# Cross-attention block on one core: softmax division after the value product, keys stacked without head masks, one GpSimd power for the inverse root

## What is computed

```python
def _layer_norm(x, g, b):
    m = jnp.mean(x, axis=-1, keepdims=True)
    v = jnp.mean((x - m) ** 2, axis=-1, keepdims=True)
    return (x - m) * jax.lax.rsqrt(v + EPS) * g + b

tgt1 = _layer_norm(tgt, g1, be1)
q, k, v = heads(tgt1 @ Wq.T + bq), heads(tgt1 @ Wk.T + bk), heads(tgt1 @ Wv.T + bv)
score = einsum('bshd,bthd->bhst', q, k) / sqrt(HD) + (1.0 - mask) * -1e9
p = softmax(score, axis=-1)
o = einsum('bhst,bthd->bshd', p, v).reshape(b, s, d)
tgt = tgt + o @ Wo.T + bo
tgt = tgt + (memory @ Wg.T + bg)
tgt1 = _layer_norm(tgt, g2, be2)
out = tgt + relu(tgt1 @ W1.T + b1) @ W2.T + b2
```

## Time and profile before

| | |
|---|---|
| three timed runs | 1951.97, 1949.45 and 1956.89 us, median 1951.97 us |
| span of the profiled execution, first to last instruction | 1947.5 us |
| busy: TensorE (PE) / VectorE (DVE) | 1804.0 us (93%) / 1812.8 us (93%) |
| busy: ScalarE (ACT) / GpSimd (POOL) | 1449.1 us (74%) / 1142.5 us (59%) |
| chain that ended last | DVE 46%, PE 20%, issue 18%, ACT 13%, rest 3% |
| mean granted TensorE clock | 0.993 of full speed |

### The profile page before, as it was taken

How to read it: one execution, slowest core, us unless ns; L and a number is a source line. 1 busy time by engine, 2 the same in 40 slices (tenths; PEclk the granted TensorE clock), 3 DMA queues, 4 the chain that set the end, 5 groups by cost and what they waited for, 6 DMA issues and landing times.

```text
span 1947.5 us, 62629 instructions
## 1 busy us (share of the span) xinstructions
PE 1804.0 (93%) x17716; PEld 1699.6 (87%) x17716; DVE 1812.8 (93%) x8535; ACT 1449.1 (74%) x5513; POOL 1142.5 (59%) x1607
## 2 busy tenths in 40 slices
PE   5899999999999999999999999999999999999997
PEld 5789889889889898898898898898898898988987
DVE  6799999999999999999999999999999999999994
ACT  4778778778777777777777787787787777777772
POOL 3556556565566566566566565665655665665663
PEclk8899999999999999999999999999999999999999
DMA  6453453453543544544544534535534435445430
GB/s 172 119 142 103 119 135 101 127 130 101 132 124 105 135 117 108 138 111 112 141 105 114 137 103 123 135 100 129 129 103 132 125 104 135 118 108 137 112 101 23
DMA packets 163903, 230.99 MB, mean 119 GB/s; under 512 B 29984, under 2 KB 114336, under 8 KB 163872
## 3 DMA queue, kind: packets, MB, share of 16 engines
q1 hardware_dynamic: 163872, 230.62, 45.5%
HBM read 62.73 MB, written 16.78 MB: 41 GB/s over the span
## 4 chain that ended last, share of the span: by engine, by line
DVE 46%; PE 20%; issue 18%; ACT 13%; DVEq 2%; POOL 1%; DMA 0%; ACTq 0%; SPq 0%; POOLq 0%
ACT scores L353 9%; DVE scores L590 9%; DVE k_hi L654 6%; DVE rstd L518 4%; DVE stats L490 4%; PE ffn_ps L772 3%; ACT hid L386 3%; PE ffn_ps L774 3%; PE ffn_ps L773 2%; PE work_ps L772 2%; DVE var L498 2%; PE work_ps L774 2%; PE work_ps L773 2%; DVE xhat L527 2%; DVE resid L564 2%
## 5 line engine op out<-in xcount | busy, mean ns | idle before, releaser
L716 POOL TENSOR_TENSOR scores<-scores,sum_inv 128x512 f32<-128x512 f32 x512 | 549.3, 1078 | 656.0 <-DVE sum_inv L533 656.0
L353 ACT ACTIVATE scores<-scores,row_min 128x128 f32<-128x128 f32 x2048 | 796.2, 397 | 184.3 <-DVE row_min L590 183.9
L590 DVE CUSTOM_DVE_ANT_0 scores<-score_ps,mask_bias 128x128 f32<-128x128 f32 x2048 | 466.0, 284 | 0.3 <-issue 0.3
L363 ACT ACTIVATE probs<-turn_ps 128x512 f32<-128x512 f32 x512 | 301.7, 590 | 187.8 <-PE turn_ps L833 187.8
L353 ACT ACTIVATION_READ_ACCUMULATOR scores<-scores,row_min 128x1 f32 x2048 | 399.7, 195 | 0.0
L833 PE MATMUL turn_ps<-ident,scores 128*128 128x128 f32 x2048 | 312.3, 275 | 31.7 <-POOL scores L716 31.6
L772 PE MATMUL ffn_ps<-w_hi,hT_lo 128*128 128x256 f32 x1024 | 304.0, 297 | 26.5 <-DVE hT_lo L634 24.6
L772 PE MATMUL ffn_ps<-zT_hi,w_lo 128*128 128x256 f32 x1024 | 304.2, 297 | 5.0 <-ACT hid L386 3.7
L722 POOL TENSOR_TENSOR hT_lo<-hid,hT_hi 128x512 fp32r<-128x512 f32 x192 | 258.3, 1345 | 70.8 <-DVE hT_hi L629 70.8
L774 PE MATMUL ffn_ps<-zT_hi,w_hi 128*128 128x256 f32 x1024 | 286.7, 280 | 0.0
L773 PE MATMUL ffn_ps<-zT_lo,w_hi 128*128 128x256 f32 x1024 | 286.4, 280 | 0.0
(11 more groups left out here) (115 smaller groups left out, 4629.5 us busy)
## 6 DMA issues: line engine op xcount, KB each, us to landing
k_stack<-k_hi SPq DMA_DIRECT2D x512, 128.0 KB, 2.8
q_stack<-q_hi SPq DMA_DIRECT2D x512, 64.0 KB, 2.0
k_stack<-k_lo SPq DMA_DIRECT2D x256, 128.0 KB, 2.8
x_in<-x_dram SPq DMA_DIRECT2D x64, 256.0 KB, 2.7
mem_in<-memory_dram SPq DMA_DIRECT2D x64, 256.0 KB, 3.4
x_res<-x_dram SPq DMA_DIRECT2D x64, 256.0 KB, 2.8
q_stack<-q_lo SPq DMA_DIRECT2D x256, 64.0 KB, 1.9
out_dram<-y SPq DMA_DIRECT2D x64, 256.0 KB, 2.4
```

The source lines that it names most:

```text
L353: last = act.activation(scores[:, k, h, :], scores[:, k, h, :], ACT.Exp, bias=row_min[:, k, h:h + 1], scale=-1.0, accum_out=row_sum[:, k, ...
L363: act.activation(probs[:, k % CPB, :], turn_ps[k % 2][:, :], ACT.Copy).then_inc(probs_copied, 1)
L590: last = dve.tensor_tensor_reduce(out=scores[:, t, h, :], in0=score_ps[t % 2][:, h * S:(h + 1) * S], in1=mask_bias[:, b, :], scale=1.0, sc ...
L716: pool.tensor_tensor(scores[:, k], scores[:, k], sum_inv[:, k, :].unsqueeze(2).broadcast_to([P, CH, S]), ALU.mult).then_inc(probs_normed, 1)
```

## The change

**Softmax division.** GpSimd no longer multiplies the eight chunks; TensorE transposes the unnormalised exponentials. VectorE inverts the sums of four chunks at once, at ticks 5 and 9. GpSimd spreads each inverse over its head's 16 columns (`inv_rows`, ticks 6 and 10). TensorE transposes these at tick 0 of the next iteration (`turn_inverses`, four more transposes). ScalarE copies them out at tick 1 (`copy_inverses`), and VectorE multiplies the value product by them at tick 2 into `attn`. The high half of `attn` is then made by ScalarE at its tick 4 and the low half by GpSimd at its tick 4.

**Keys.** `kk` has one copy of the keys. ScalarE writes the high half straight from PSUM, VectorE the low half. `k_stack` is zeroed once as a whole, and SyncE copies 16 partitions at a time, so that the other head's rows stay zero: 24 DMAs an iteration in place of 12. The v product waits for `k_split` now.

**Inverse root.** One GpSimd add and one GpSimd power with -0.5 for each norm. The Newton steps and seeds are gone from both engines.

**Moved.** The memory's split goes from VectorE tick 1 to GpSimd tick 2, the fourth hidden low half from VectorE to GpSimd, the bias of the residual from GpSimd tick 4 to 6, and that of the result from tick 2 to 0.

```diff
-INVERT_TICKS = (1, 2, 3, 5, 5, 7, 7, 9)
-NORM_TICKS = (1, 2, 3, 5, 6, 7, 8, 9)
+INVERT_TICKS = (5, 9)
...
                     for r in range(CPB):
-                        for j, high_low in enumerate((0, 1, 0)):
-                            sp.dma_start(k_stack[32 * j:32 * j + 32, r].bitcast(F32),
-                                         kk[high_low][32 * r:32 * r + 32].bitcast(F32)
-                                         ).then_inc(k_stacked[r], 16)
+                        for e in range(2):
+                            at = 32 * r + HD * e
+                            for j, high_low in enumerate((0, 1, 0)):
+                                to = 32 * j + HD * e
+                                sp.dma_start(k_stack[to:to + HD, r, :, e, :].bitcast(F32),
+                                             kk[high_low][at:at + HD].rearrange("p k (b s) -> p (k b) s", b=GB)
+                                             .bitcast(F32)).then_inc(k_stacked[r], 16)
...
+            def copy_inverses(g):
+
+                act.wait_ge(inv_turned, g + 1)
+                if later(g):
+                    act.wait_ge(attn_ready, g)
+                act.activation(inv[:].rearrange("p k r -> p (k r)"), turn_ps[0][:, :], ACT.Copy
+                               ).then_inc(inv_copied, 1)
...
+                    if out_ and t == 1:
+                        copy_inverses(i - 1)
+                    if out_ and t == 4:
+                        g = i - 1
+                        split_high(attn[:], attnT[0], attn_ready, g + 1, proj_ready,
+                                   g if later(g) else None, attnT_hi)
...
                     if out_ and t == 2:
                         g = i - 1
                         dve.wait_ge(attended, GB * (g + 1))
+                        dve.wait_ge(inv_copied, g + 1)
                         if later(g):
-                            dve.wait_ge(proj_ready, g)
-                        dve.tensor_copy(attnT[0][:], value_tiles).then_inc(attnT_hi, 1)
-                        split_low(value_tiles, attnT, attnT_hi, g + 1, attnT_split)
+                            dve.wait_ge(attnT_split, g)
+                        dve.tensor_tensor(attn[:], value_tiles, inv[:], ALU.mult).then_inc(attn_ready, 1)
...
+                pool.tensor_tensor(var[:], mv[:, :, 1], eps[:], ALU.add).then_inc(var_done, 1)
+                pool.wait_ge(var_done, g + 1)
+                pool.tensor_tensor(rstd[:], var[:], minus_half[:], ALU.pow).then_inc(done, 1)
...
+                    if out_ and t == 4:
+                        split_low(attn[:], [a[:] for a in attnT], attnT_hi, i, attnT_split)
...
-                pe.wait_ge(probs_normed, CHUNKS * g + k + 1)
+                pe.wait_ge(exps_ready, CHUNKS * g + k + 1)
...
+            def turn_inverses(g):
+
+                pe.wait_ge(inv_spread, GB * (g + 1))
+                pe.wait_ge(probs_copied, CHUNKS * g + CHUNKS - 1)
+                for k in range(KT):
+                    for b in range(GB):
+                        last = pe.transpose(turn_ps[0][:, k * ROWS + b * S:k * ROWS + (b + 1) * S],
+                                            inv_rows[:, b, k, :], ident[:])
+                last.then_inc(inv_turned, 1)
```

More of the change, by code:

```diff
@@ L192, in xattn_block @@
         xres_loaded, y_stored = sem("xres_loaded"), sem("y_stored")
-        ln1_stats, ln1_mean, ln1_var, ln1_half, ln1_seed, ln1_ready = (
-            sem(f"ln1_{n}") for n in ("stats", "mean", "var", "half", "seed", "ready"))
+        ln1_stats, ln1_mean, ln1_var, ln1_rstd, ln1_ready = (
+            sem(f"ln1_{n}") for n in ("stats", "mean", "var", "rstd", "ready"))
         x_turned, x_hi, x_split = sem("x_turned"), sem("x_hi"), sem("x_split")
         q_ready, q_high, q_split = sem("q_ready"), sem("q_high"), sem("q_split")
-        k_ready, k_copied, k_high, k_split = sem("k_ready"), sem("k_copied"), sem("k_high"), sem("k_split")
+        k_ready, k_high, k_split = sem("k_ready"), sem("k_high"), sem("k_split")
         zeros_set = sem("zeros_set")
@@ L210, in xattn_block @@
         proj_ready, xres_biased, resid_ready = sem("proj_ready"), sem("xres_biased"), sem("resid_ready")
-        ln2_stats, ln2_mean, ln2_var, ln2_half, ln2_seed, ln2_ready = (
-            sem(f"ln2_{n}") for n in ("stats", "mean", "var", "half", "seed", "ready"))
+        ln2_stats, ln2_mean, ln2_var, ln2_rstd, ln2_ready = (
+            sem(f"ln2_{n}") for n in ("stats", "mean", "var", "rstd", "ready"))
         z_turned, z_hi, z_split = sem("z_turned"), sem("z_hi"), sem("z_split")
-        ln1_step, ln1_rstd, ln2_step, ln2_rstd = (sem(n) for n in ("ln1_step", "ln1_rstd", "ln2_step", "ln2_rstd"))
         hid_ready, hid_relu, hid_hi, hid_split = (sem(f"s_hid_{n}") for n in ("ready", "relu", "hi", "split"))
@@ L493, in layer_norm_stats @@
                 dve.wait_ge(stats_done, g + 1)
+                if later(g):
+                    dve.wait_ge(rstd_done, g)
                 for b in range(GB):
@@ new lines, in inverse_root, with spread_inverses @@
+            def inverse_root(g, mv, var, rstd, mean_done, var_done, ready, done):
+                pool.wait_ge(mean_done, g + 1)
+                if later(g):
+                    pool.wait_ge(ready, g)
+                pool.tensor_tensor(var[:], mv[:, :, 1], eps[:], ALU.add).then_inc(var_done, 1)
+                pool.wait_ge(var_done, g + 1)
+                pool.tensor_tensor(rstd[:], var[:], minus_half[:], ALU.pow).then_inc(done, 1)
+            def spread_inverses(g, b):
+                pool.wait_ge(sums_inverted, GB * g + b + 1)
+                if later(g):
+                    pool.wait_ge(inv_turned, g)
+                pool.tensor_tensor(inv_rows[:, b].rearrange("p k (h d) -> p (k h) d", d=HD),
+                                   sum_inv[:, b].rearrange("p k c e -> p (k c e)").unsqueeze(2)
+                                   .broadcast_to([P, H, HD]),
+                                   one[:, :].unsqueeze(2).broadcast_to([P, H, HD]), ALU.mult
+                                   ).then_inc(inv_spread, 1)
@@ L710, in iteration, with split_low @@
+            def split_low(src, halves, high, count, done):
+                pool.wait_ge(high, count)
+                pool.tensor_tensor(halves[1], src, halves[0], ALU.subtract).then_inc(done, 1)
             def iteration(i, norm, front, attn_, out_, ffn):
                 for t in range(TICKS):
-                    if attn_ and t in NORM_TICKS:
-                        k = NORM_TICKS.index(t)
-                        pool.wait_ge(sums_inverted, CHUNKS * i + k + 1)
-                        pool.tensor_tensor(scores[:, k], scores[:, k],
-                                           sum_inv[:, k, :].unsqueeze(2).broadcast_to([P, CH, S]),
-                                           ALU.mult).then_inc(probs_normed, 1)
@@ new lines, in iteration @@
+                    if attn_ and t == 6:
+                        spread_inverses(i, 0)
+                    if attn_ and t == 10:
+                        spread_inverses(i, 1)
+                    if out_ and t == 2:
+                        g = i - 1
+                        pool.wait_ge(mem_loaded, 16 * (g + 1))
+                        if later(g):
+                            pool.wait_ge(proj_ready, g)
+                        pool.tensor_tensor(memT[0][:], mem_in[:],
+                                           one[:, 0:1].unsqueeze(2).broadcast_to([P, KT, ROWS]), ALU.mult
+                                           ).then_inc(mem_hi, 1)
+                        split_low(mem_in[:], [m[:] for m in memT], mem_hi, g + 1, mem_split)
@@ L729, in iteration @@
+                    if out_ and t == 6:
                         if is_at(i, 1):
@@ L734, in iteration @@
                                            ALU.add).then_inc(xres_biased, 1)
[L735 removed]
+                    if ffn and t == 0:
                         g = i - 2
@@ L827, in turn_chunk @@
             def turn_chunk(g, k):
-                pe.wait_ge(probs_normed, CHUNKS * g + k + 1)
+                pe.wait_ge(exps_ready, CHUNKS * g + k + 1)
+                if k == 0 and later(g):
+                    pe.wait_ge(inv_copied, g)
                 if k >= 2 or later(g):
```

160 lines of the change are left out of this document (50 added, 110 removed).

## The result

| | before | after |
|---|---|---|
| median | 1952.05 us (4 runs, 1949.45 to 1956.89) | 2150.76 us (4 runs, 2148.19 to 2151.56) |
| ratio, 95% interval | | 1.101 (1.0991 to 1.103) |
| span of the profiled execution | 1947.5 us | 2149.7 us |
| mean granted clock | 0.993 | 0.964 |

The change makes the kernel 10% slower. The direction was forecast; the time lies 61 us above the upper end of the range.

A forecast was written before the change was run, and what follows sets the result against it. TensorE, waiting 2.73 us an iteration for the attention output, bounds the kernel: 42 (longer iteration) + 30 (clock) + 0 (key DMAs) + 4 (ends) = 76 us on 1947.5, giving a 2028 us median; range 1958 to 2090.

The forecast's parts named there:

- The attention output's long way: Halves by ScalarE, then GpSimd, ready 13.69 us after X; TensorE's projection waits 2.73; +0.70 us an iteration, 42 in all.
- X: Start of TensorE's transposes of xhat at tick 0, the point each iteration's times are counted from.
- VectorE's relief and TensorE alone: VectorE sheds 9 to 10 us an iteration and is no bound; TensorE alone needs 27.48 us with four more transposes.
- the four old waits: TensorE's four waits in an iteration of the kernel before, for VectorE or what hangs on it: 2.31 us together.
- The clock: TensorE's wait before the projection lowers its clock: 0.5 us an iteration, between 0 and 1.5; 30 us in all.
- Rival D: The clock falls in every iteration at the wait before the projection, costing 1.5 us instead of 0.5; 2088 us; chance 0.12.
- SyncE issues 24 key DMAs: I cost it at nothing: In SyncE's queue, the fourth key block lands 5.0 us after X; no cost, margin 0.4, at most 24 us.
- rival C: SyncE decides: if a key DMA issue takes over 0.75 us, TensorE waits for keys; about 2063 us at 0.80; chance 0.12.
- The power: GpSimd's power for each norm takes between 0.41 and 3 us; nothing gained or lost.
- The ends: First key stacking takes 7.7 us longer, iterations without all stages have shorter VectorE lists: +4 us.
- Rival A: Attention output comes in time; TensorE with SyncE's queue gives 28.95 us an iteration, about 1922 us in all; chance 0.12.

The follow-up runs named there:

- e3_both: The change with both attention output halves made on VectorE and the key part undone (12 key DMAs): 1831.6 us, ratio 0.9398 to before.
- e8_filler: e2_keys12 with 22 dummy products on TensorE just before its wait for the attention output: 1987.6 us, ratio 1.0182 to before.
- e2_keys12: The change with the key part alone undone: masked key copies on VectorE, 12 key DMAs of 128 KB; 2028.8 us, ratio 1.0411 to before.
- e5_keys_alone: The kernel before with the key part alone: 24 key copies of 16 partitions, no masked copies on VectorE; 1973.2 us, ratio 1.0108.
- e1_attn_dve: The change with both attention output halves on VectorE at its tick 2, key DMAs still 24: 2011.6 us, ratio 1.0318 to before.
- e7_newton_back: e3_both with the seeds and three Newton steps back in place of the GpSimd power: 2132.8 us, ratio 1.0924 to before.

## Why the prediction was right or wrong

**The attention output's long way: right.** With the key part taken out, the kernel took 2028.8 us, where 2028 was forecast. TensorE waited for `attnT_lo` up to 2.6 us (2.73 forecast). The projection came in that kernel 12.51 us after the copy of xT, and that copy starts 0.74 after X in the earlier trace rows, so 13.25 against 13.69. Over 28 iterations, from the copy of xT at 1005.98 to that at 1866.98, the period was 861.0/28 = 30.75; the forecast had 30.21 plus 0.5. That the two times agree within 1 us is luck: the iterations without a fall took 29.86, 0.35 less than the 30.21, and the falls cost that much more than the 0.5.

**VectorE's relief and TensorE alone: right.** The forecast was 27.48; `e3_both` runs at 27.6 with TensorE 98% busy, with the four old waits gone.

**The clock: right in kind, too small.** 0.5 us an iteration was taken, 30 us in all, between 0 and 1.5. The filled wait gave back 41. The falls come in about every second iteration and cost 1.7 us each. Rival D is rejected in its form of every iteration. The forecast quoted the Trainium skill (TensorE: Matmul & The Clock Gate, PE-mode transpose) that transposes don't count as a busy engine. `e8_filler` keeps the four transposes ahead of the wait and those at X, and its mean clock is 0.995: here the transposes alone brought no fall.

**"SyncE issues 24 key DMAs: I cost it at nothing": this step failed.** The prices in it held. The starts are 0.64 apart, so rival C's condition of more than 0.75 never came true; yet its picture, TensorE waiting for `k_stack`, did, by another route. What failed is that the start of the keys was counted as a fixed 8.16 us after the queries. That is true only while the third and fourth query blocks don't wait. They wait for the seventh and eighth score products, which stand behind the projection that the same prediction made late. In the change the keys start 1030.83 - 1020.25 = 10.58 after the queries, 2.42 later than counted, against a margin of 0.4.

The second fault is in the same step: a loss of 0.2 at the fourth score product was set off "out of the 2.73 it must wait anyway". A later fourth score product doesn't eat into that wait. Past the margin of 0.4 it makes the key product late, then ScalarE's list, then the projection, by about as much. In the change the fourth score product comes 6.33 after X, where 5.0 was counted, and the projection 14.78 after X, where 13.69 was (X is at 1009.74). The forecast took its own loop from X to X as closed and never followed the projection through SyncE's queue to the keys and back, which is loop 1. Price of the step: 122 us, where the bound given was 24.

**The power: right.** It takes 0.70 us, between the bounds of 0.41 and 3. VectorE waits for it for 1.9 us in all. I had not seen that in the new order the Newton steps would cost far more than before.

**The ends: too small.** They were put at +4 and cost 29 (see the copies of xT above). With 12 key copies (`e2_keys12`) they cost 6, so some 23 of the 122 us of the failed step lie at the ends, outside loop 1. `e5_keys_alone` has the same 22. The forecast counted the longer queue once, for the first stacking; why each end pays more I have not traced.

**Rival A** did not happen, since the attention output came late. `e1_attn_dve` fulfils its condition and still takes 2011.6, not 1922: 28.95 an iteration was counted and 30.2 came, since loop 2 holds the halves that went back to VectorE. That `e3_both` reaches 1831.6 shows that there was some 120 us to gain. The change lost that and 199 us more.

## What to carry to other kernels

A queue that never waits by itself can be the bound if its first entry waits for something that its last entry releases. So for each late piece, follow its successors into the DMA queue and around to itself, and sum the loop, instead of checking the slack of each piece once. Then check that each step really waits for the one before: every walk around sums to the period, but only one without slack explains it. When a change relieves the busiest engine by giving work to others, ask where that work stands in their strict lists: here two halves of the right size, late in two lists, cost 197 us with 12 key copies, and back on the relieved engine, then 88% busy, they leave TensorE no wait. Try the parts of such a change apart: two of them taken back turned +10% into -6%.

## What the runs showed of the hardware

- A DMA start from SyncE between SBUF tiles takes 0.64 us of its queue, the same for 32, 64 and 128 KB (the earlier trace rows and the rows above). Halving the size of the copies and doubling their count therefore doubles the queue's time. The landing takes 2.0 us for 32 and 64 KB, 2.8 for 128 KB.
- GpSimd's power on 128x2 takes 0.70 us. In `e7_newton_back` one of its small multiplies takes 0.20, with 0.27 from one to the next when they depend on each other.
- In `e2_keys12` a single wait of 2.0 us in an otherwise full TensorE brought the clock from 2.4 to 1.2 GHz for 3.4 us, and only about every second time. Filling it with useless products gained 41 us, 2%.
